# GRU over conditioned attention: input tiles turned by VectorE's 32x32 blocks from a second, blocked copy in memory, instead of by TensorE

## What is computed

```python
def attention_layer(x, emb):                     # emb = cond[:, None, :]
    scale, shift = split(emb @ W_emb + b_emb)
    xn = rms_norm(x, g_norm) * (1 + scale) + shift
    q, k, v = heads(xn @ W_qkv)                  # 16 heads of 32
    q, k = rms_norm(q, g_q), rms_norm(k, g_k)
    o = softmax(q @ k.T * 32 ** -0.5) @ v
    return o + o @ W_out

def cell(h, x):                                  # GRU, h starts as cond
    gi, gh = x @ W_ih + b_ih, h @ W_hh + b_hh
    r, z = sigmoid(gi_r + gh_r), sigmoid(gi_z + gh_z)
    n = tanh(gi_n + r * gh_n)
    return (1 - z) * n + z * h

x1 = x + attention_layer(x, cond)
out = x1 + scan_over_256_steps(cell, cond, x1)
```

## Time and profile before

| | us |
|---|---|
| median of 3 runs | 1779.7 |
| the profiled execution, its own time | 1782.16 |
| its span, first to last instruction | 1780.4 |
| TensorE busy | 1729.3 (97%) |
| VectorE busy | 1109.6 (62%) |
| ScalarE busy | 998.1 (56%) |
| GpSimd busy | 395.0 (22%) |
| DMA queue of SP | 25.0% of 16 engines |

### The profile page before, as it was taken

One profiled execution on the slowest core, in us unless ns is written; L12 is line 12 of the kernel. 1 busy time (PEld: TensorE's weight loads), 2 busy tenths in 40 slices (PEclk: granted clock), 3 DMA queues, 4 the chain that ended last, 5 costly groups with the idle time before them and its releaser, 6 DMA issues.

```text
span 1780.4 us, 68426 instructions
## 1 busy us (share of the span) xinstructions
PE 1729.3 (97%) x28841; PEld 1392.8 (78%) x28841; DVE 1109.6 (62%) x4016; ACT 998.1 (56%) x3615; POOL 395.0 (22%) x481
## 2 busy tenths in 40 slices
PE   6899999999999998999999999999999999999986
PEld 5688888888888886688878878888788888888875
DVE  4677676677767766355556656656556656565664
ACT  4777777777777775244444444444444444444444
POOL 4533333344343333011111111111111111111111
PEclk9999999999999999999999999999999999999999
DMA  5021111111111105623323333333233333332320
GB/s 219 1 107 49 39 46 37 37 37 37 37 37 46 39 25 124 113 62 77 78 72 77 77 76 76 75 77 79 72 77 77 74 77 76 77 78 67 71 65 14
DMA packets 130522, 119.37 MB, mean 67 GB/s; under 512 B 9932, under 2 KB 108440, under 8 KB 130216
## 3 DMA queue, kind: packets, MB, share of 16 engines
q1 hardware_dynamic: 130216, 115.00, 25.0%
HBM read 73.01 MB, written 41.94 MB: 65 GB/s over the span
## 4 chain that ended last, share of the span: by engine, by line
PE 93%; DMA 2%; POOL 1%; DVE 1%; issue 1%; ACT 1%; SPq 0%; POOLq 0%; DVEq 0%
PE ps L635 38%; PE ps L606 19%; PE ps L422 14%; PE ps L468 6%; PE ps L504 5%; PE ps L449 4%; PE ps L483 3%; PE ps L430 2%; PE ps L514 1%; PE ps L404 1%; PE ps L491 1%; POOL rq L1136 1%; DMA xres<-in_x_dram 1%; DMA wemb<-in_L_cond_W_emb_dram 0%; DMA wout<-in_L_cond_W_out_dram 0%
## 5 line engine op out<-in xcount | busy, mean ns | idle before, releaser
L635 PE MATMUL ps<-whh,hT 128*32 128x192 f32 x16384 | 718.5, 327 | 17.4 <-DVE hT L893 17.4
L635 PEld LDWEIGHTS ps<-whh,hT 128*32 128x32 f32 x16384 | 595.8, 110 | 132.1 <-issue 67.6
L606 PE MATMUL ps<-wih,x1T 128*32 128x256 f32 x6144 | 388.7, 380 | 1.1 <-ACT x1T L989 0.7
L1080 ACT ACTIVATE v<-ps 128x128 f32<-128x128 f32 x512 | 139.7, 273 | 430.2 <-PE ps L635 430.2
L1197 POOL TENSOR_TENSOR outG<-hG,GI 128x128 f32<-128x128 f32 x256 | 117.3, 458 | 958.4 <-DVE hG L886 958.4
L867 DVE SCALAR_TENSOR_TENSOR v<-v,ps 128x64 f32<-128x64 f32 x512 | 113.3, 221 | 331.5 <-ACT v L1080 331.5
L606 PEld LDWEIGHTS ps<-wih,x1T 128*32 128x32 f32 x6144 | 229.9, 110 | 74.9 <-issue 6.1
L969 ACT ACTIVATE P<-ps,nmx 128x256 f32<-128x256 f32 x512 | 236.9, 483 | 1.9 <-DVE nmx L695 1.9
L1088 ACT ACTIVATE v<-v 128x64 f32<-128x64 f32 x512 | 131.3, 256 | 107.0 <-DVE v L872 107.0
L1136 POOL TENSOR_TENSOR rq<-msq,mh 128x16 f32<-128x16 f32 x64 | 185.7, 2902 | 5.5 <-POOL msq L1132 0.2
L695 DVE TENSOR_REDUCE nmx<-ps 128x4 f32<-128x1024 f32 x128 | 156.2, 1221 | 29.4 <-PE ps L449 29.4
(11 more groups left out here) (94 smaller groups left out, 1970.3 us busy)
## 6 DMA issues: line engine op xcount, KB each, us to landing
gscr<-nat SPq DMA_DIRECT2D x96, 256.0 KB, 2.6
GI<-gscr SPq DMA_DIRECT2D x128, 192.0 KB, 3.7
xb<-in_x_dram SPq DMA_DIRECT2D x16, 512.0 KB, 3.6
xres<-in_x_dram SPq DMA_DIRECT2D x32, 256.0 KB, 2.9
xscr<-x1s SPq DMA_DIRECT2D x32, 256.0 KB, 2.0
x1n<-xscr SPq DMA_DIRECT2D x32, 256.0 KB, 2.7
GI<-xscr SPq DMA_DIRECT2D x128, 64.0 KB, 2.7
out_dram<-outG SPq DMA_DIRECT2D x128, 64.0 KB, 2.9
```

Source lines behind the costliest of these rows:

```text
L606: last = pe.matmul(F[G % 2][q, n], x1T[:, tt % 2, c, q], wih[:, c, g * D + 256 * half:g * D + 256 * half + 256], start=(c == 0), stop=(c = ...
L635: last = pe.matmul(ps[32 * j:32 * j + 32, q, 0:192], hT[:, 32 * c:32 * c + 32], whg[:, c, :, 128 * j + 64 * q:128 * j + 64 * q + 64], star ...
L1080: s.activation(v_rz[:, q, :], ps[:, q, 64:192], ACT.Tanh, scale=0.5).then_inc(s_tr, 1)
```

## The change

Besides `xscr` the kernel stores every half of `x1` a second time, to `xblk`, in which the 512 features of a row stand in another order: group a (of 4) holds features 32a to 32a + 31 of each of the four chunks of 128. SP issues this as four DMAs per half, whose runs in SBUF are 32 features (128 bytes) long. `out_sum` on VectorE now waits for these stores too. A tile for the gates is then loaded with four DMAs, one for each 32 partitions, so that partitions 32a to 32a + 31 hold the rows in four groups of 32 beside one another, with the features of group a. One VectorE transpose of 128x512, by 32x32 blocks, leaves `x1T` with the features on the partitions, now laid out. TensorE's transposes and ScalarE's copies of tiles 1 to 31 are gone; tile 0 still goes the old way, from `xscr`. In the recurrence, VectorE turns the next tile in the seventh step of each tile, behind that step's `turn_h(1)`, and SP issues the four loads of a later tile (`tt + 5`) in its seventh and eighth step.

```diff
+    xblk = nc.dram_tensor("xblk", [T, NB, D], F32, kind="Internal").ap()
...
-        x1T = sb("x1T", [128, 2, KC, 128])
+        x1T = sb("x1T", [128, 2, 4, KC, 32])
...
+            def store_blocks(b, i):
+
+                emptied(sp, ("out", b, i))
+                for a in range(4):
+                    sp.dma_start(xblk[128 * i:128 * i + 128, b, 128 * a:128 * a + 128].rearrange("t (c k) -> t c k", c=KC),
+                                 x1s.rearrange("p (c a k) -> p a c k", c=KC, a=4)[:, a]).then_inc(s_xb[i], 16)
...
+            def load_blocks(tt, a):
+
+                if a == 0:
+                    sp.wait_ge(s_xb[tt // (NT // 2)], 64 * NB)
+                    if tt == 2:
+                        sp.wait_ge(s_1T, 1)
+                    elif tt > 2:
+                        sp.wait_ge(s_1c, tt - 2)
+                sp.dma_start(x1n[tt % 2][32 * a:32 * a + 32, :].rearrange("p (r f) -> p r f", r=4),
+                             xb_v[tt, :, 128 * a:128 * a + 128].rearrange("(r p) f -> p r f", r=4)).then_inc(s_xl[tt % 2], 16)
...
                 if b:
                     store_x1(b - 1, 0)
                     load_residual(b - 1, 1)
+                    store_blocks(b - 1, 0)
...
                 if b:
                     store_x1(b - 1, 1)
                 load_residual(b, 0)
+                if b:
+                    store_blocks(b - 1, 1)
             store_x1(NB - 1, 0)
             load_residual(NB - 1, 1)
             load_x1(0)
-            load_x1(1)
+            store_blocks(NB - 1, 0)
             sp.wait_ge(s_bz, 9)
             for j in range(4):
                 load_gx(0, j)
-            load_x1(2)
+            for tt in range(1, 3):
+                for a in range(4):
+                    load_blocks(tt, a)
...
-            load_x1(4)
+            for a in range(4):
+                load_blocks(4, a)
+            store_blocks(NB - 1, 1)
...
+                if s >= 6 and tt + 5 < NT:
+                    load_blocks(tt + 5, 2 * s - 12)
+                    load_blocks(tt + 5, 2 * s - 11)
...
-                turn_x1(tt + 1, F[2])
...
-                    if turned:
-                        turn_x1(pt + 1, F[2])
...
                 if i:
                     v.wait_ge(s_xo[0], 16 * (b + 1))
+                    v.wait_ge(s_xb[0], 64 * (b + 1))
                 elif b:
                     v.wait_ge(s_xo[1], 16 * b)
+                    v.wait_ge(s_xb[1], 64 * b)
...
+            def turn_blocks(tt):
+
+                v.wait_ge(s_xl[tt % 2], 64 * (tt // 2 + 1) if tt % 2 else 16 + 64 * (tt // 2))
+                v.transpose(x1T[:, tt % 2].rearrange("p r c t -> p (r c t)"), x1n[tt % 2]).then_inc(s_1c, 1)
...
                     keep_gate(tt, g, F[(3 * tt + g) % 2])
+                    if tt == 0 and g == 0:
+                        turn_blocks(1)
                 if tt == 0:
+                    turn_blocks(2)
                     out_sum(NB - 1, 1)
...
                 for pt, g, k, turned in pieces(t):
+                    if turned:
+                        turn_blocks(pt + 1)
                     if k == GP - 1:
                         keep_gate(pt, g, F[(3 * pt + g) % 2])
...
-            for tt in range(3):
-                x1_keep(tt, F[2])
+            keep_first_x1(F[2])
...
-                for pt, g, k, turned in pieces(t):
-                    if turned:
-                        x1_keep(pt + 1, F[2])
```

More of the change, by code:

```diff
@@ L221, in cond_resid_kernel @@
         s_xo = [sem("x1_out0"), sem("x1_out1")]
+        s_xb = [sem("x1_blocks_out0"), sem("x1_blocks_out1")]
         s_bz, s_bb, s_b0, s_lwh, s_lwi = (sem(n) for n in ("pool_setup", "bn_load", "h0_load", "whh", "wih"))
-        s_1T, s_1c, s_g, s_gb, s_sd = (
-            sem(n) for n in ("x1_turned", "x1_kept", "gate", "gate_kept", "seeded"))
+        s_1T, s_1k, s_1c, s_g, s_gb, s_sd = (
+            sem(n) for n in ("first_x1_turned", "first_x1_kept", "x1_blocks_turned", "gate", "gate_kept", "seeded"))
         s_xl, s_st, s_gl, s_out = ([sem(f"{n}{e}") for e in range(2)] for n in ("x1_load", "gate_out", "gate_in", "h_out"))
@@ L242, in _ @@
             x_v = xscr.rearrange("(t s) b d -> t (s b) d", s=ST)
+            xb_v = xblk.rearrange("(t s) b d -> t (s b) d", s=ST)
             x_j = xscr.rearrange("(t s) b (j f) -> t j b s f", s=ST, j=4)
@@ L259, in store_x1 @@
                 sp.dma_start(xscr[128 * i:128 * i + 128, b, :], x1s).then_inc(s_xo[i], 16)
-            def x1_there(tt):
-                sp.wait_ge(s_xo[tt // (NT // 2)], 16 * NB)
+            def store_blocks(b, i):
[3 more added lines that the diff above has]
+                                 x1s.rearrange("p (c a k) -> p a c k", c=KC, a=4)[:, a]).then_inc(s_xb[i], 16)
             def load_x1(tt):
-                x1_there(tt)
-                if tt >= 2:
-                    sp.wait_ge(s_1T, tt - 1)
+                sp.wait_ge(s_xo[0], 16 * NB)
                 sp.dma_start(x1n[tt % 2], x_v[tt]).then_inc(s_xl[tt % 2], 16)
+            def load_blocks(tt, a):
[7 more added lines that the diff above has]
+                             xb_v[tt, :, 128 * a:128 * a + 128].rearrange("(r p) f -> p r f", r=4)).then_inc(s_xl[tt % 2], 16)
             def gi_free(tt):
@@ L346, in _ @@
             store_x1(NB - 1, 1)
-            load_x1(3)
+            for a in range(4):
+                load_blocks(3, a)
             for g in range(3):
@@ L376, in _ @@
                             load_gates(tt + 1, s - 2)
+                if s >= 6 and tt + 5 < NT:
+                    load_blocks(tt + 5, 2 * s - 12)
+                    load_blocks(tt + 5, 2 * s - 11)
                 for pt, g, k, turn in pieces(t):
-                    if turn and pt + 3 < NT:
-                        load_x1(pt + 3)
                     if k == GP - 1:
@@ L387, in _ @@
                 sp.wait_ge(s_xo[e], 16 * NB)
+                sp.wait_ge(s_xb[e], 64 * NB)
         @block.tensor
@@ L506, in out_proj, with turn_first_x1 @@
                 last.then_inc(s_op, 1)
-            def turn_x1(tt, bank):
+            def turn_first_x1(bank):
                 v = bank.rearrange("p (c t) -> p c t", c=KC)
-                pe.wait_ge(s_xl[tt % 2], 16 * (tt // 2 + 1))
-                if tt:
-                    pe.wait_ge(s_1c, tt)
+                pe.wait_ge(s_xl[0], 16)
                 for c in range(KC):
-                    last = pe.transpose(v[:, c, :], x1n[tt % 2][:, 128 * c:128 * c + 128], ident)
+                    last = pe.transpose(v[:, c, :], x1n[0][:, 128 * c:128 * c + 128], ident)
                 last.then_inc(s_1T, 1)
@@ L598, in gate_piece @@
                 if k == 0:
-                    pe.wait_ge(s_1c, tt + 1)
+                    if tt:
+                        pe.wait_ge(s_1c, tt)
+                    else:
+                        pe.wait_ge(s_1k, 1)
                     if G >= 2:
@@ L605, in gate_piece @@
                     q = slice(32 * j, 32 * j + 32)
-                    last = pe.matmul(F[G % 2][q, n], x1T[:, tt % 2, c, q], wih[:, c, g * D + 256 * half:g * D + 256 * half + 256],
+                    last = pe.matmul(F[G % 2][q, n], x1T[:, tt % 2, j, c, :], wih[:, c, g * D + 256 * half:g * D + 256 * half + 256],
                                      start=(c == 0), stop=(c == KC - 1), skip_group_check=True)
@@ L612, in _ @@
             emptied(pe, ("recips", NP - 1))
-            turn_x1(0, F[2])
+            turn_first_x1(F[2])
             for tt in range(2):
@@ L983, in keep_turned_p, with keep_first_x1 @@
                 s.copy(PT[:, U % 2, 0:2, :, :], pP[:, 0:2, :, :]).then_inc(s_pa, 1)
[L985 to L989, removed]
+            def keep_first_x1(bank):
+                s.wait_ge(s_1T, 1)
+                s.copy(x1T[:, 0].rearrange("p r c t -> p c r t"), bank.rearrange("p (c r t) -> p c r t", c=KC, r=4)).then_inc(s_1k, 1)
             def wq_high(g):
```

## The result

| | before | after |
|---|---|---|
| median, us | 1780.14 (4 runs, 1778.99 to 1781.44) | 1764.93 (4 runs, 1761.56 to 1766.31) |
| profiled execution, its span | 1782.16, 1780.4 | 1766.31, 1764.4 |
| TensorE busy | 1729.3 | 1710.8 |
| VectorE busy | 1109.6 | 1128.0 |
| ScalarE busy | 998.1 | 978.9 |

The ratio is 0.9905, 95% interval 0.9893 to 0.9917. With the fourth run of before its median is 1780.1 in place of 1779.7.

A forecast was written before the change was run, and what follows sets the result against it. It took the recurrence's loop TensorE, ScalarE, VectorE, TensorE as the bound, with transposes lengthening only the step that turns a tile. -20.3 + 3.5 + 1.7 = -15.1 us gave a median of 1764.6 us, range 1758.5 to 1771.

The forecast's parts named there:

- Part 1: Recurrence and just ahead of it: taking x1's transposes off TensorE saves 19.1 and 1.2 us, together 20.3 us.
- C: Recurrence, seventh step: VectorE's block transpose takes 1.94 us, adding 15.4 us; 1780.0 us, no change; chance 0.05.
- D: Recurrence: the step that turns a tile doesn't shorten, something else takes its place; 1783.7 us, slower; chance 0.04.
- Part 2: Recurrence, seventh step: VectorE's block transpose takes 0.68 us, hidden in 1.41 us of waiting, so it costs nothing.
- Part 3: Between the phases: the last sequence's out_sum waits for the second store, at 27 ns a packet, +3.5 us (0.9 to 7).
- Rival B: Between the phases: at 135 ns a run the copy takes 17.3 us and delays tile 1; 1785.7 us, slower; chance 0.05.
- Rival E: Between the phases: short runs are cheap (7 ns) and TensorE's clock holds; 1760.3 us; chance 0.18.
- rival A: Between the phases: short runs cost double (54 ns) and the clock stays low longer; 1769.8 us; chance 0.18.
- Part 4: Between the phases: TensorE's longer second stall brings one more 3.4 us low-clock stretch, half of it counted, +1.7 us.
- Part 5: Between the phases: tile 1's blocks are turned at 721.3, 5 us before TensorE wants them, so they cost nothing.

The follow-up runs named there:

- e4: The change with each block transpose of tiles 3 to 31 done twice, once into a spare buffer; 1765.67 us, ratio to before 0.9907.
- e5: The change with each block transpose of tiles 3 to 31 done three times; 1773.68 us, ratio to before 0.9955.
- e9: The kernel before plus only the second store and its waits, with five float32 matmuls in TensorE's stall between the phases; ratio to before 1.0009.
- e11: The change run once more, unaltered, for another profile; 1764.91 us in one run.
- e3: The change with five float32 matmuls put into TensorE's stall ahead of the last probabilities; 1763.07 us, ratio to before 0.9891.
- e2: The change without the second store and its waits, tile loads reading xscr instead; 1762.34 us, ratio to before 0.9890.
- e8: The e7 kernel with the second half of the recurrent weights loaded behind the blocks of tiles 1 and 2; 1768.20 us, ratio to before 0.9928.
- e6: The change with two sum buffers, one for each half; 1762.60 us, ratio to before 0.9889.
- e1: The kernel before with only the second store of x1 and out_sum's waits added, nothing reading the copy; 1786.43 us, ratio to before 1.0020.
- e7: The change with two sum and two residual buffers, the last sequence's first residual loaded ahead of the recurrent weights; 1759.59 us, ratio to before 0.9877.

## Why the prediction was right, and where its terms were not

**The time.** 1764.6 us predicted, 1764.93 measured, against a median of before that moved up by 0.4: -15.1 against -15.2. That the two agree to 0.1 us is luck: terms of the sum were wrong by 2 and 3 us, in opposite directions.

**Part 1 was right, a little small.** 29 x 0.662 = 19.2 us and the two groups ahead of the recurrence (the first `out_proj` and tile 1's gates now follow at once) are as forecast. The recurrence gained 20.2: common steps went from 3.970 to 3.967 us, some 0.6 in all, and the irregular second and fourth step took 0.4 less. Rivals C and D fell: the transpose takes 0.67 us and the seventh step 3.97.

**Part 2 was right.** 0.67 us against 0.68, with 0.82 us left; e4 and e5 show that the cover was what hid it.

**Part 3 had the right place and half the price.** The step was "I take 27, the packet of the nearest size at its whole price". The short packet takes 13 ns, so 128 of them are 1.7 us, not 3.5, and the sum waited 1.4 us longer (13.74 - 12.34; e9 gives 1.4 alone). At a packet every 10.6 ns it would be 128 x 10.6 = 1.4 us. SP's four issues took 8.29 us there and not the 1.85 that was counted. The Trainium skill (DMA: Bandwidth & Descriptors, Specifications) gives 512 bytes as the least transfer for the full rate and a read, modify and write below it. The loss of rate shows here: a quarter of the bytes took half the time, about twice the time per byte. The prediction's reading of it, that a short packet costs twice a long one, is not borne out. Rival B, which needed 110 ns, is out. Rival E had a better price (7 ns) but a clock that holds, rival A the longer low clock but a price of 54 ns.

**Part 4 had the right mechanism and was too small.** "One more such stretch of 3.4 us" was 13.7 us in the profiled execution and in e11, 10.2 in e4 and e5. By e3 the low clock is worth 4.3 us up to the first tanh, against 1.7 forecast. It stayed low while TensorE was busy 8.29 of 9 us, which the row of before, where it came back after 3.4, had not suggested. Its premise, a fall behind a stall of 1.73 us, isn't dependable either: in the profile after, the same stall of 1.72 us at 698.68 was followed by no fall. Nor is the second stall the copy's alone: it was 3.2 us without the copy (e2), because the first low stretch, which had shortened it in before, isn't there in every execution; "that second stall grows to 5.2 us" held for executions without it (4.67 to 4.85), and was 2.9 to 3.0 with it.

**Part 5 was right.** The last of tile 1's blocks landed at 718.67, and VectorE turned the tile at 722.47, right behind the first kept gate, with no wait. What came nearer to the chain was the way back of tile 0's gates: they landed at 741.06, 1.0 us ahead of the first seed (2.3 us before), and in e8 they were the limit.

So +5.0 us between the phases came from -1.2, +1.4 and, as what is left, +4.8 in place of -1.2, +3.5 and +1.7: two errors of opposite sign, 2 and 3 us. Of the +4.8, e3 takes away 4.3; the other 0.5 isn't accounted for. By the medians the change is slower by about 0.15% than without the wait for the copy (e2, e6) and by 0.14% than with TensorE kept busy (e3), each with overlapping intervals. Clear of the noise is only the whole cost of the copy in the kernel of before, 0.20% (e1, 0.10 to 0.29). What stays open is why stalls alike in length (4.67 and 4.63, or 2.95 and 2.92 us) are followed by a long stretch in one execution and by a short one or none in another. That a stall as such is needed is what e3 and e9 show, with one profile each.

## What to carry to other kernels

Measure a step with and without the work in question before counting an engine's busy share as its bound: here TensorE was 97% busy, and only one step in eight had anything to give. Work moved to VectorE was free as long as it fitted in that engine's wait in that step, and repeating the operation there is a cheap test of where the edge is. This change's side costs gathered where the program changes phase: look for the single buffer behind a long transfer. A second sum buffer and a second residual buffer together took 0.28%, 5 us, off the change (e7); that is more than the 0.14% of e3, though the intervals of e7 and e3 overlap. A sum that comes out can hide terms that don't: check each term against its own row.

## What was not expected of the hardware

- Runs of 128 bytes move in 13 ns a packet, half the 27 ns of 512 bytes, and overlap, with up to 1515 packets in 1 us on the 16 DMA engines.
- A DMA issue on SP that normally takes 0.43 us took 4.93 (4.05 to 5.16 in the seven other profiles with the copy at that place) when 3 MB of weights were under way and the issues before it had many short runs. In e6, where the copy stands behind the loads of tiles 1 and 2, its longest issue took 1.44 us.
- The lower clock level lasted up to 13.7 us behind a stall of 4.7 us, over 8.29 us of work in 9, and behind a stall as long (4.63 us) in the copy-alone kernel 3.4 us. Stalls of 2.9 to 3.2 us were followed by 10.2 us, 3.4 us or nothing.
